# A graph layer with residual norm on one core: product chunks spread over the row schedule, u prepared in pieces, last products in three pieces

## The chip, the core and the metric

The kernel runs on one core of a Trainium2 chip. TensorE does matmuls and transposes into PSUM; VectorE, ScalarE and GpSimd work on data in SBUF and, the first two, in PSUM; SyncE and ScalarE issue DMAs. The metric is the device time of one execution in microseconds (us).

## What is computed

For each of 8 batches, with N = 2048 nodes and C = 64 channels (the adjacency `W` is 2048 x 2048 in float32, 16 MB per batch):

```python
Ws = 0.5 * (W + jnp.swapaxes(W, -1, -2))
A = jax.nn.sigmoid(U @ U.T)              # U: 2048 x 16, one for all batches
K = Ws * A[None, :, :]
deg = jnp.maximum(K.sum(axis=-1), EPS)
d = jax.lax.rsqrt(deg)
K = K * d[:, :, None] * d[:, None, :]
g = w_scale * jnp.einsum('bnm,bmc->bnc', K, x)
out = _layernorm(x + g, axis=-1)
```

## The kernel before

**Tiling.** A batch's adjacency is cut into 16 units of 512 x 512 (1 MB); unit (i, j) lies in SBUF as `K[(i, j)]`, 128 partitions x 4 chunks x 512. K is symmetric, so only ten blocks are worked out (`STEPS`: the diagonal ones and those below), of four rows of 128 each: 40 rows per batch, numbered 0 to 39. Rows of a diagonal block are 128, 256, 384 and 512 columns wide, all others 512.

**A row.** For each pair of rows TensorE transposes the mirrored unit into PSUM `tw` (four banks; 16 instructions for a full pair, 6 or 14 on the diagonal; `transpose_adjacency`, line 349). VectorE adds `tw` to the unit (line 572) and, one row behind, multiplies by the gate A and sums the row for the degree (line 583). Six rows later or so, TensorE transposes the finished rows back for the mirrored half into PSUM `kt` (two banks, line 362, both used by each pair of rows), and ScalarE copies them out with their row sums (line 489: a copy of 0.6 us and a readout of the sum). The next `kt` transposes wait for these copies (`upper_done`); those of a block's first two rows also wait for VectorE to be done with the block (`lower_done`).

**Products.** When the degrees of a group of nodes are known (`DEG_ROWS`, a power on GpSimd) and x is scaled by d (`Z_ROWS`, tile z), TensorE multiplies: eight pairs of units (`PAIRS`), each with four chunks, and a chunk is two matmuls over 512 columns, of 64 x 512 outputs side by side, each of which runs as two instructions. The 32 chunks of a batch accumulate in the two banks of `yp`. The output is copied, transposed, scaled, x is added, and mean, centring, square, variance and division make the norm, in four parts on GpSimd, beside the rows of the following batches.

**What sets the order.** Each engine runs a list written out by row. Tables of clocks say where each piece of side work stands: a clock c of batch b means row c mod 40 of batch b + c // 40. So `PRODUCT_ROWS` = 41 is row 1 of the next batch. On TensorE a row holds, in this order, the `tw` transposes (even rows), the y transposes, the products of that row, and the `kt` transposes (even rows). The first batch has in addition, per two rows, three outer products of u with three sigmoids (lines 416 and 480), which make the gate A that stays in SBUF.

**Loads.** SyncE's queue loads the next batch's units pair by pair; a pair's load waits until the pair's last product is done (`prod_done`, line 215), since the products are the last readers. Rows 4, 12, 16 and 28 are the first to add into (1,0), (2,0), (3,0) and (3,2). `STORE_PAIR` says behind which pair's loads the output store of the batch before the previous one stands.

**Start and end.** Before row 0, u is split into high and low parts in `stack_a` and `stack_b` (lines 698 and 704) and transposed in eight groups through eight PSUM banks (line 452), copied by VectorE and ScalarE (709, 546). After the last batch's row 39 TensorE does what is left of the products (line 469): pairs whose last chunk has a clock of 40 or more. Bank 0 is finished first, and its norm (`finish_last`, lines 662 to 690) runs while bank 1's products are done; bank 1's norm then runs alone.

## Time and profile before

| | us |
|---|---|
| median of three runs | 531.81 (526.47 to 533.03) |
| the profiled execution | 527.15 |
| its span in the profile | 525.3 |
| TensorE busy | 433.0 (82%) |
| VectorE busy | 421.1 (80%) |
| ScalarE busy | 210.2 (40%) |
| GpSimd busy | 118.4 (23%) |
| DMA | 143.08 MB, mean 272 GB/s |

The span leaves out 1.85 us of the execution's time. Busy times are those in which at least one instruction of the engine runs; a matmul's end is modelled, so TensorE's busy share is somewhat too large. A row of the timeline gives start, duration, engine, line, operation, output and input tiles, shapes and count, and in square brackets how long the engine had stood idle before it and what released it.

### The profile page before, as it was taken

Reading aid. Unit: us, or ns where it says so; the run is one execution under the profiler, and the core shown is the slowest. Engines: PE = TensorE matmul, PEld = TensorE weight load, DVE = VectorE, ACT = ScalarE, POOL = GpSimd, SP = SyncE. Lnnn points to the kernel's source line nnn. Section 1 sums busy time; section 2 is a strip of 40 time slices with the busy share of each in tenths; the row PEclk is TensorE's granted clock in tenths of the full one; section 3 lists DMA queues with packets and bytes.
Section 4 is the critical chain, followed back from the end, with each engine's and each line's share of the span. In section 5 each row is a group of like instructions: output and inputs, shape, how many; then the busy total and the mean of one; then the engine's idle time right before and its main releaser. Section 6 shows DMA issues by size and latency. Waiting matters only on the chain.

```text
span 525.3 us, 14322 instructions
## 1 busy us (share of the span) xinstructions
PE 433.0 (82%) x5256; PEld 235.8 (45%) x5256; DVE 421.1 (80%) x1137; ACT 210.2 (40%) x654; POOL 118.4 (23%) x132
## 2 busy tenths in 40 slices
PE   4887789787888789798888789788898889787791
PEld 4555434454445443554345434454354544554230
DVE  5788746999779978999779968899779977999333
ACT  3697421454224531453234531453234541454200
POOL 0000000004410254004410244004410244004611
PEclk9799899999999999999999989999999999999797
DMA  8996569984999689994999669995999679990011
GB/s 281 387 356 240 182 230 365 353 264 168 351 381 285 202 298 357 338 337 167 329 393 307 222 239 353 340 340 190 325 384 309 224 278 371 339 326 0 1 41 40
DMA packets 102857, 143.08 MB, mean 272 GB/s; under 512 B 37296, under 2 KB 37296, under 8 KB 102832
## 3 DMA queue, kind: packets, MB, share of 16 engines
q1 hardware_dynamic: 88240, 139.08, 75.1%
q10 hardware_dynamic: 14592, 3.67, 3.3%
q8 instruction: 16, 0.26, 0.2%
q14 instruction: 9, 0.07, 0.1%
HBM read 138.54 MB, written 4.19 MB: 272 GB/s over the span
## 4 chain that ended last, share of the span: by engine, by line
PE 60%; ACT 11%; issue 10%; DMA 9%; DVE 7%; SPq 1%; POOLq 0%; POOL 0%; DVEq 0%; ACTq 0%
PE yp L387 35%; PE kt L345 13%; ACT k L489 9%; DMA out_dram<-h 7%; PE tw L345 7%; PE yp L469 3%; DVE k L572 2%; DVE k L583 2%; PE yp L416 2%; DMA k<-in_adj_dram 2%; ACT gate L480 1%; SPq L203 1%; DMA h<-in_L_gnn_U_dram 1%; DVE h L619 1%; PE tw L452 1%
## 5 line engine op out<-in xcount | busy, mean ns | idle before, releaser
L489 ACT ACTIVATE k<-kt 128x512 f32<-128x512 f32 (+3 forms) x288 | 149.6, 524 | 266.3 <-PE kt L345 266.2
L572 DVE TENSOR_TENSOR k<-tw,k 128x512 f32<-128x512 f32 (+2 forms) x320 | 193.3, 604 | 66.2 <-PE tw L345 56.2
L387 PE MATMUL yp<-k,z 128*64 128x512 f32 x928 | 219.5, 610 | 0.6 <-issue 0.4
L583 DVE CUSTOM_DVE_ANT_0 k<-k,gate 128x512 f32<-128x512 f32 (+2 forms) x320 | 202.4, 633 | 0.3 <-ACT gate L480 0.3
L345 PE MATMUL kt<-ident,k 64*128 64x64 f32 x1920 | 93.5, 229 | 70.7 <-ACT k L489 61.5
L345 PEld LDWEIGHTS kt<-ident,k 64*128 64x128 f32 x1920 | 76.2, 140 | 99.7 <-issue 99.4
L387 PEld LDWEIGHTS yp<-k,z 128*64 128x64 f32 x928 | 61.3, 139 | 100.3 <-issue 95.8
L345 PEld LDWEIGHTS tw<-ident,k 64*128 64x128 f32 x2176 | 82.7, 140 | 49.9 <-issue 49.8
L345 PE MATMUL tw<-ident,k 64*128 64x64 f32 x2176 | 100.2, 228 | 1.7 <-DMA k<-in_adj_dram 0.9
L277 POOL TENSOR_TENSOR d<-deg,minus_half 128x4 f32<-128x4 f32 x32 | 34.3, 1071 | 254.4 <-DVE deg L593 254.2
L489 ACT ACTIVATION_READ_ACCUMULATOR k<-kt 128x1 f32 x288 | 57.2, 199 | 0.0
L253 POOL TENSOR_TENSOR h<-h,x_keep 128x256 f32<-128x256 f32 x28 | 24.0, 880 | 52.6 <-DVE deg_parts L583 52.6
L265 POOL TENSOR_TENSOR rstd<-var,minus_half 128x16 f32<-128x16 f32 x7 | 20.3, 2899 | 23.2 <-DVE var L633 23.2
L583 DVE DVE_READ_ACCUMULATOR2_ANT deg_parts<- 128x1 f32 x320 | 25.5, 80 | 0.0
L259 POOL TENSOR_TENSOR h<-h,mean 128x256 f32<-128x256 f32 x28 | 19.3, 696 | 26.6 <-DVE deg_parts L583 15.0
L469 PE MATMUL yp<-k,z 128*64 128x512 f32 x96 | 23.5, 650 | 0.0
L270 POOL TENSOR_TENSOR h<-h,rstd 128x256 f32<-128x256 f32 x28 | 17.0, 612 | 26.3 <-DVE deg_parts L583 26.2
L480 ACT ACTIVATE gate<-yp 128x512 f32<-128x512 f32 (+3 forms) x40 | 19.9, 535 | 4.4 <-PE yp L416 4.2
L416 PE MATMUL yp<-ut_b,ut_a 128*128 128x512 f32 (+3 forms) x40 | 16.6, 470 | 2.0 <-ACT gate L480 1.7
L603 DVE TENSOR_TENSOR z<-xt,d 128x256 f32<-128x256 f32 x32 | 15.5, 484 | 2.3 <-POOL d L277 2.2
L469 PEld LDWEIGHTS yp<-k,z 128*64 128x64 f32 x96 | 7.2, 149 | 14.8 <-issue 14.7
L669 DVE TENSOR_TENSOR k<-tw,f 128x512 f32<-128x512 f32 x2 | 1.4, 692 | 14.3 <-PE tw L398 14.3
(60 smaller groups left out, 130.4 us busy)
## 6 DMA issues: line engine op xcount, KB each, us to landing
k<-in_adj_dram SPq DMA_DIRECT2D x128, 1024.0 KB, 7.2
xt<-in_x_dram ACTq DMA_DIRECT2D x7, 512.0 KB, 5.9
out_dram<-h SPq DMA_DIRECT2D x7, 512.0 KB, 8.9
xt<-in_x_dram SPq DMA_DIRECT2D x1, 512.0 KB, 13.9
out_dram<-k SPq DMA_DIRECT2D x2, 256.0 KB, 2.6
h<-in_L_gnn_U_dram SPq DMA_DIRECT2D x1, 128.0 KB, 3.9
ws<-in_L_gnn_w_scale_dram ACTq DMA_DIRECT2D x1, 0.5 KB, 3.3
```

Source lines behind the costliest of these rows:

```text
L253: nc.gpsimd.tensor_tensor(h[:, part(k), :], h[:, part(k), :], x_keep[:, part(k), :], ALU.add).then_inc(h_ready, 1)
L259: nc.gpsimd.tensor_tensor(h[:, part(k), :], h[:, part(k), :], per_row(mean, part(k).start, part(k).stop), ALU.add).then_inc(centered, 1)
L265: nc.gpsimd.tensor_tensor(rstd[:, :], var[:, :], minus_half[:, :], ALU.pow).then_inc(rstd_ready, 1)
L277: nc.gpsimd.tensor_tensor(d[:, s], deg[:, s], minus_half[:, s], ALU.pow).then_inc(d_ready, 1)
L345: t = pe.transpose(dst[h][:, at + k * H:at + (k + 1) * H], block[H * h:H * h + H, :], ident[H * h:H * h + H, H * h:H * h + H])
L387: t = pe.matmul(yp[at:at + C, m // 2, :], z[:, n * G + c, :], K[(n, m)][:, c, :], start=(q == first_unit[m] and c == 0), stop=(q == last_u ...
L416: pe.matmul(yp[:, g % 2, 0:w], ut_a[:, (i * G + r) * P:(i * G + r + 1) * P], ut_b[:, j * UW:j * UW + w], start=True, stop=True).then_inc(u ...
L469: t = pe.matmul(yp[at:at + C, m // 2, :], z[:, n * G + c, :], K[(n, m)][:, c, :], start=False, stop=(q in (LAST_BANK0 - 1, NQ - OWN - 1) a ...
L480: nc.scalar.activation(A[:, A_AT[g]:A_AT[g] + w], yp[:, g % 2, 0:w], ACT.Sigmoid).then_inc(gate_ready, 1)
L489: nc.scalar.activation(K[(j, i)][:, r, c0:UW].rearrange("p (c h e) -> p c h e", h=2, e=H), whole_rows(kt[:, 0:2, :], r % 2, (UW - c0) // P ...
L572: nc.vector.tensor_tensor(row, whole_rows(tw[:, tw_bank[g] // 2 * 2:tw_bank[g] // 2 * 2 + 2, :], g % 2, w // P), row, ALU.add).then_inc(su ...
L583: nc.vector.tensor_tensor_reduce(row, row, A[:, A_AT[g]:A_AT[g] + w], 1.0, 0.0, ALU.mult, ALU.add, deg_parts[:, i * G + r, j:j + 1]).then_ ...
```

## The change

1. `PRODUCT_ROWS`: the 32 chunks stood in ten places (rows 29, 31, 37, 41, 45, 48, 53, 57, 62, 64); now in nineteen: 29, 32, 33, 35, 38, 39, 42, 44, 45, 46, 47, 50, 52, 54, 56, 59, 61, 64 and 65. The last chunk of pairs 0 to 7 moves from 31, 37, 41, 45, 48, 48, 57, 64 to 32, 35, 39, 45, 46, 52, 56, 65. The other tables of clocks move by up to five rows, `KEEP_ROW` (which also issues the next x load) by six, and the store stands behind pair 5's loads.
2. u is loaded with four neighbouring rows in each partition (256 bytes in a piece instead of 64), split quarter by quarter, and only the first quarter is transposed ahead of row 0; the others stand at rows 0, 1 and 2 of the first batch, all through `kt`. Fourteen transposes of the identity stand first on TensorE, one sigmoid of one column first on ScalarE.
3. Three pairs instead of two end before clock 40, so five instead of six are left for the end. They are done in three pieces: bank 0; the first half of bank 1's columns; the second half, which goes to a `kt` bank and is added to the copied earlier sum. Each piece has its own norm and two stores, the last on two queues.

```diff
-PRODUCT_ROWS = [29, 29, 31, 31, 37, 37, 37, 37, 41, 41, 41, 41, 45, 45, 45, 45, 45, 45, 48, 48, 48, 48, 48, 48, 53, 53, 57, 57, 62, 62, 62, 64]
-DEG_ROWS = [25, 34, 40, 43]
-Z_ROWS = [26, 37, 43, 45]
-KEEP_ROW = 61
+PRODUCT_ROWS = [29, 29, 32, 32, 33, 33, 35, 35, 38, 38, 39, 39, 42, 44, 44, 45, 45, 45, 46, 46, 46, 47, 50, 52, 54, 56, 56, 56, 59, 61, 64, 65]
+DEG_ROWS = [25, 32, 40, 43]
+Z_ROWS = [26, 35, 43, 44]
+KEEP_ROW = 55
...
-STORE_PAIR = 6
+STORE_PAIR = 5
...
+UT_ROWS = [0, 0, 1, 2]
+WARM = 14
...
+PIECES = [(0, 0, G), (1, 0, G // 2), (1, G // 2, G)]
+PIECE_Y_AFTER = 5
...
-            sp.dma_start(u_sb, u.rearrange("(n p) r -> p n r", p=P)).then_inc(h_moved, 16)
+            sp.dma_start(u_sb, u.rearrange("(g p n) r -> p g n r", p=P, n=G)).then_inc(h_moved, 16)
...
+            def transpose_u(k):
+
+                pe.wait_ge(stack_ready, 1 if k == 0 else 2)
+                for e, src in ((2 * k, stack_a), (2 * k + 1, stack_b)):
+                    if e - KT_RING >= 0:
+                        before = e - KT_RING
+                        pe.wait_ge((ut_a_copied, ut_b_copied)[before % 2], before // 2 + 1)
+                    for n in range(G):
+                        t = pe.transpose(kt[:, e % KT_RING, n * P:(n + 1) * P], src[:, k, n, :], ident[:, :])
+                    t.then_inc(ut_done, 1)
...
+            for k in range(WARM):
+                pe.transpose(tw[:, k % TW_RING, 0:P], ident[:, :], ident[:, :])
+            transpose_u(0)
             steps(0, 1)
...
+            for piece, (k, c0, c1) in enumerate(PIECES):
+                columns = slice(c0 * P, c1 * P)
+                chunks = [(pair, c) for pair in LAST_PAIRS[k] for c in range(G)]
+                for at, (pair, c) in enumerate(chunks):
+                    if piece and at == PIECE_Y_AFTER:
+                        transpose_last_y(piece - 1)
+                    if piece == 0 and c == 0 and PAIRS.index(pair) in Z_OF_PAIR:
+                        pe.wait_ge(z_ready, NZ * (B - 1) + (Z_OF_PAIR[PAIRS.index(pair)] + 1))
                     for n, m in pair:
...
+                        half = (m % 2) * C
+                        y = last_sums(piece)[half:half + C, :]
+                        t = pe.matmul(y, z[:, n * G + c, :], K[(n, m)][:, c, columns],
+                                      start=(c0 > 0 and at == 0), stop=(at == len(chunks) - 1))
+                t.then_inc(last_done, 1)
+            transpose_last_y(len(PIECES) - 1)
...
+            act.wait_ge(ident_ready, 1)
+            nc.scalar.activation(warm[:, :], ident[:, 0:1], ACT.Sigmoid)
+            copy_u(0)
...
+            def join_last_y(piece):
+
+                dve.wait_ge(last_done, piece + 1)
+                dve.wait_ge(y_copied, 2 * B - 2 + piece)
+                y = piece_of(K[(0, 0)], piece)
+                nc.vector.tensor_tensor(y, last_sums(piece), y, ALU.add).then_inc(y_copied, 1)
```

Two places on TensorE show the move. The first is rows 32 to 38 of a steady batch: `tw` and `kt` are the two kinds of transposes, `yp<-k,z` are products, four instructions in this list being two chunks of two matmuls. Before:

```order
L345 MATMUL tw<-ident,k 128x64 x6
L345 MATMUL kt<-ident,k 128x64 x16
L345 MATMUL tw<-ident,k 128x64 x14
L345 MATMUL kt<-ident,k 128x64 x16
L345 MATMUL tw<-ident,k 128x64 x6
L345 MATMUL kt<-ident,k 128x64 x16
L387 MATMUL yp<-k,z 64x512 x8
```

and of the change:

```order
L395 MATMUL tw<-ident,k 128x64 x6
L437 MATMUL yp<-k,z 64x512 x4
L395 MATMUL kt<-ident,k 128x64 x16
L437 MATMUL yp<-k,z 64x512 x4
L395 MATMUL tw<-ident,k 128x64 x14
L395 MATMUL kt<-ident,k 128x64 x16
L437 MATMUL yp<-k,z 64x512 x4
L395 MATMUL tw<-ident,k 128x64 x6
L395 MATMUL kt<-ident,k 128x64 x16
```

Three groups of two chunks now stand between and beside the `kt` transposes that followed each other before, and the group of four chunks of row 37 is gone (it has become those of rows 33 and 35).

The second is the end, after the loop: the last `kt` transposes, the products (with `64x256` half as wide) and the y transposes (`tw<-ident,k 128x128`). Before:

```order
L345 MATMUL kt<-ident,k 128x64 x14
L469 MATMUL yp<-k,z 64x512 x28
L398 MATMUL tw<-ident,k 128x128 x4
L469 MATMUL yp<-k,z 64x512 x20
L398 MATMUL tw<-ident,k 128x128 x4
```

and of the change:

```order
L395 MATMUL kt<-ident,k 128x64 x14
L535 MATMUL yp<-k,z 64x512 x16
L535 MATMUL yp<-k,z 64x256 x10
L449 MATMUL tw<-ident,k 128x128 x4
L535 MATMUL yp<-k,z 64x256 x14
L535 MATMUL kt<-k,z 64x256 x10
L449 MATMUL tw<-ident,k 128x128 x2
L535 MATMUL kt<-k,z 64x256 x14
L449 MATMUL tw<-ident,k 128x128 x2
```

The 48 matmuls over 512 columns have become 16 over 512 and 48 over 256, and what follows the last of them has half the columns.

## Rows read from the trace of the kernel before

**Rows 1.** The page, part 1: busy us (share of the span) xinstructions.
```profile
PE 433.0 (82%) x5256; PEld 235.8 (45%) x5256; DVE 421.1 (80%) x1137; ACT 210.2 (40%) x654; POOL 118.4 (23%) x132
```

**Rows 2.** Waits over the span: us in total, times, longest.
```profile
PE kt L345 <- ACT k L489: 61.5, 71, 1.4
DVE k L572 <- PE tw L345: 56.2, 42, 5.2
...
DVE k L572 <- DMA k<-in_adj_dram: 9.5, 13, 1.9
```

**Rows 3.** Busy time by stretch of one steady batch, rows 32 to 15, then 16 to 31.
```profile
core 0: us, PE busy (x) PEld busy (x) DVE busy (x) ACT busy (x) POOL busy (x), PEclk, DMA share, GB/s
359.16:395.87 36.71, 31.23 (x364) 15.74 (x362) 30.04 (x89) 12.65 (x45) 14.88 (x16) 1.00 0.91 330
395.87:417.59 21.72, 19.09 (x295) 11.64 (x292) 21.34 (x54) 10.79 (x31) 1.01 (x1) 1.00 0.82 263
```

**Rows 4.** Timeline, VectorE's adds of rows 10, 12, 29 and 30.
```profile
387.80 0.56 DVE L572 TENSOR_TENSOR k<-tw,k 128x384 f32<-128x384 f32 x1 [1.81 <-PE tw L345]
...
390.45 0.69 DVE L572 TENSOR_TENSOR k<-tw,k 128x512 f32<-128x512 f32 x1 [0.53 <-DMA k<-in_adj_dram]
...
413.95 0.68 DVE L572 TENSOR_TENSOR k<-tw,k 128x512 f32<-128x512 f32 x1
...
415.17 0.68 DVE L572 TENSOR_TENSOR k<-tw,k 128x512 f32<-128x512 f32 x1
```

**Rows 5.** Timeline, TensorE and its weight loads (PEld) at six places.
```profile
381.75 5.37 PE L387 MATMUL yp<-k,z 128*64 128x512 f32 x24
...
387.05 0.14 PEld L345 LDWEIGHTS kt<-ident,k 64*128 64x128 f32 x2 [0.81 <-issue]
...
396.79 0.58 PEld L345 LDWEIGHTS tw<-ident,k 64*128 64x128 f32 x16 [0.81 <-issue]
...
397.37 0.61 PEld L345 LDWEIGHTS kt<-ident,k 64*128 64x128 f32 x16
...
419.14 0.71 PE L345 MATMUL kt<-ident,k 64*128 64x64 f32 x16 [1.01 <-ACT k L489]
...
421.31 0.72 PE L345 MATMUL kt<-ident,k 64*128 64x64 f32 x16 [1.26 <-ACT k L489]
...
421.95 3.65 PE L387 MATMUL yp<-k,z 128*64 128x512 f32 x16
```

**Rows 6.** A 2 us stretch of full loading (columns as rows 3).
```profile
376.00:378.00 2.00, 2.00 (x12) 0.65 (x10) 1.58 (x6) 0.00 (x0) 2.00 (x1) 1.00 1.05 409
```

**Rows 7.** Line 203, the adjacency loads, from issue to landing.
```profile
DMA to landing us min/median/max: 5.0/7.2/16.3
```

**Rows 8.** The page, part 6: the load of u, KB, median us to landing.
```profile
h<-in_L_gnn_U_dram SPq DMA_DIRECT2D x1, 128.0 KB, 3.9
```

**Rows 9.** Timeline of the start, ScalarE.
```profile
12.62 1.28 ACT L480 ACT_TABLE_LOAD   x1
...
13.92 0.55 ACT L480 ACTIVATE gate<-yp 128x128 f32<-128x128 f32 x2
```

**Rows 10.** The stretch from 490 to 500 us (columns as rows 3).
```profile
490.00:500.00 10.00, 10.00 (x36) 2.98 (x37) 2.21 (x6) 1.24 (x3) 6.23 (x6) 0.76 0.01 2
```

**Rows 11.** Timeline of the end.
```profile
489.82 14.71 PE L469 MATMUL yp<-k,z 128*64 128x512 f32 x56
...
491.58 0.24 PEld L469 LDWEIGHTS yp<-k,z 128*64 128x64 f32 x2 [0.62 <-issue]
...
494.93 0.14 PEld L469 LDWEIGHTS yp<-k,z 128*64 128x64 f32 x2 [0.55 <-issue]
...
509.82 4.03 PE L469 MATMUL yp<-k,z 128*64 128x512 f32 x18
...
515.25 0.69 DVE L669 TENSOR_TENSOR k<-tw,f 128x512 f32<-128x512 f32 x1 [2.86 <-PE tw L398]
...
519.99 1.64 POOL L327 TENSOR_TENSOR rstd<-var,minus_half 128x8 f32<-128x8 f32 x1 [8.32 <-DVE var L687]
```

More of the change, by code:

```diff
@@ L88, in upper_row_of @@
     return (s + 1) * G + r + UPPER_LAG
+FIRST_STEP_OF_ROWS = [min(s for s in range(len(STEPS)) if STEPS[s][0] == i) for i in range(G)]
 def gates_before(row):
@@ L98, in due @@
     return clock == NL * lag + row
-LAST_PAIRS = [n for n in PAIRS[OWN:] if n[0][1] == 0] + [n for n in PAIRS[OWN:] if n[0][1] != 0]
-LAST_BANK0 = sum(n[0][1] == 0 for n in PAIRS[OWN:])
-LAST_Y_CHUNK = 2
+LAST_PAIRS = [[n for n in PAIRS[OWN:] if n[0][1] // 2 == k] for k in range(2)]
+PIECES = [(0, 0, G), (1, 0, G // 2), (1, G // 2, G)]
+PIECE_Y_AFTER = 5
 def bass_graph_resnorm_kernel(nc, x, adj, u, w_scale, out):
@@ L382, in product @@
                         pe.wait_ge(gate_ready, NL)
-                    elif q < 2 and not first:
-                        pe.wait_ge(y_scaled, 2 * b + (q - 1))
+                    elif q in FIRST_PAIR_OF_BANK and not first:
+                        pe.wait_ge(y_scaled, 2 * b + (FIRST_PAIR_OF_BANK.index(q) - 1))
                 for n, m in PAIRS[q]:
@@ L437, in steps @@
                     if lags == 1:
+                        for k in range(1, G):
+                            if UT_ROWS[k] == row:
+                                transpose_u(k)
                         for g in range(gates_before(row), gates_before(row + 1)):
@@ L534, in steps @@
                     if lags == 1:
+                        for k in range(1, G):
+                            if UT_ROWS[k] == row:
+                                copy_u(k)
                         for g in range(gates_before(row), gates_before(row + 1)):
@@ L654, in steps @@
                     add_row(b, g)
+                    if lags == 1:
+                        for k in range(1, G):
+                            if UT_ROWS[k] == g:
+                                copy_u(k)
                     if g:
@@ L693, in _ @@
             nc.vector.memset(deg_parts[:, :, :], 0.0)
[L694 to L695 removed]
+            nc.vector.memset(stack_a[:, :, :, 4 * R:P], 0.0)
+            nc.vector.memset(stack_b[:, :, :, 4 * R:P], 0.0)
             dve.wait_ge(h_moved, 16)
[L697 to L698 removed]
@@ L711, in _ @@
+            copy_u(0)
             steps(0, 1)
@@ L729, in _ @@
             dve.wait_ge(f_ready, B)
-            for k in range(2):
-                finish_last(k)
+            for piece in range(len(PIECES)):
+                if PIECES[piece][1] > 0:
+                    join_last_y(piece)
+                last_center(piece)
+                if piece:
+                    last_divide(piece - 1)
+                last_var(piece)
+            last_divide(len(PIECES) - 1)
 _INS = ["x", "adj", "L0_gnn_U", "L0_gnn_w_scale"]
```

212 lines of the change are left out of this document (122 added, 90 removed).

## The prediction

> **What bounds the kernel now.** The page first: TensorE is busy for 82% of the 525.3 us span and VectorE for 80% [rows 1]; neither is a plain bound, so the waits come next. Over the span TensorE waits 61.5 us for ScalarE's copies out of kt, VectorE 56.2 us for TensorE's tw and 9.5 us for adjacency loads [rows 2]. The two engines wait for each other, at different places. I then cut one steady batch out by VectorE's rows, from its first add of row 32 to the same add a batch later: 58.43 us, VectorE busy 51.38, TensorE 50.32 (the sums of the two stretches in [rows 3]). In rows 16 to 31 (21.72 us) VectorE is busy 21.34: that stretch is VectorE's own work. In row 32 to row 15 of the next batch (36.71 us) VectorE is busy 30.04 and idles 6.67. So any gain in steady state must come out of these 6.67 us; below 51.4 us a batch VectorE is the bound.
>
> The timeline says who takes them [rows 4]: 1.81 us at row 10, behind the 24 product matmuls of row 8, and 0.53 us at row 12 for a load; four such waits for TensorE and two for loads make up the stretch. On TensorE the same stretch has three kt transposes in a row at rows 32, 34 and 36 with nothing but 14 or 6 short transposes between them; each stands about 1.0 to 1.3 us until ScalarE has emptied kt [rows 5]. So TensorE idles first and is overloaded directly after: the products stand in few, large groups at the wrong places.
>
> **What the change does, part by part.**
>
> *Products.* A chunk (four matmul instructions) is worth 0.86 us: the group of 24 starts at 381.75 and the next kt weight load at 387.05, 5.30 us for six [rows 5]; so a group costs 0.86 per chunk and about 0.14 once for leaving it. Entering costs about 0.1: from a kt group to its product group 0.64 us pass (421.31 to 421.95), from one transpose group of 16 to the next 0.58 or less (396.79 to 397.37). The change makes 19 groups out of 10, so TensorE gets 9 x 0.25 = 2.2 us more to do per batch, 50.3 -> 52.5.
>
> Against that stand the waits for ScalarE, 8 us in this batch (the two in [rows 5] are of nine). In the new order two chunks stand between the kt groups of rows 30, 32, 34 and 36, and one chunk or more ahead of those of rows 2, 6, 10 and 14. ScalarE needs about 1.4 us for two rows of kt (419.14 + 0.71 to 421.31); two chunks and a tw group take more, so these waits go, all but a few tenths at row 8.
>
> I walk stretch 32 to 16 with these prices: 0.55 per 16 transposes (0.22 and 0.48 for 6 and 14), 0.86 per chunk, the 0.25 per group, 1.21 us of VectorE per full row (413.95 to 415.17, [rows 4]), VectorE's small operations at their new rows, and TensorE ahead by some 3 us at row 32 (it has 1.1 us of work in rows 30 and 31, against 3.0 before). TensorE then reaches the tw of row 34 at 2.0 us (VectorE stands 0.2), of row 36 at 4.7 (0.5), of row 0 at 10.3 (1.0), of row 6 at 18.5 (none), of row 8 at 23.0 (1.3). VectorE begins row 12 at 26.4 and, unhindered, row 16 at 31.2.
>
> *Loads.* A unit of 1 MB takes 2.6 us at the 409 GB/s of a full stretch [rows 6]; from the data's start to the first unit's landing it is 3.6 us, and from issue about 1.5 us more (the shortest landing is 5.0, [rows 7]). The new places free pair 0 a row later, pairs 1, 2 and 4 two rows sooner, pair 5 four rows later. By the walk (1,0) lands at 15.1 us, when row 4 wants it at 14.8 (stall 0.35); (2,0) lands at 26.4, just when row 12 starts. But (3,0) is freed by the chunk at row 12, at 27.2; it lands at 32.3, and row 16 wants it at 31.2: a new stall of 1.1 us. These stalls add up to 4.4 us. VectorE's work in the stretch is 27.9 us by unit prices (eight full rows 9.7, four diagonal blocks of 3.2, small operations 5.4), 30.0 by the trace [rows 3]; the difference is time in which GpSimd works beside it, and part of that will fall into the stalls. So row 16 comes between 32.3 us (all of it absorbed) and 34.4 (none); I take 33.6, nearer the second, since the measured stretch is the sum of both (30.0 + 6.7). Gain 36.7 - 33.6 = **3.1 us per batch, 21.7 for seven**.
>
> Rows 16 to 31 stay at 21.7: VectorE has the same work there. (3,2) is freed at row 25 instead of 24 and needed at row 28, 6.3 us of VectorE's work later against 5 to 5.5 to landing: no cost, without much left. The output store moves ahead of the loads of pair 6: SP waits there for the divide of row 14, two rows ahead of pair 6's last product, so nothing behind it on SP is late. The x load, now issued at row 15 from ScalarE's queue, comes after (3,0) has its data.
>
> *The start.* Before, all eight groups of u transposes and their copies stand ahead of row 0, and ScalarE loads its sigmoid table only then, at 12.62, for 1.28 us, with the first gate behind it at 13.92 [rows 9]. Now only the first quarter of u is split and transposed ahead of row 0, and the table is loaded while u is on its way. VectorE still splits all four quarters before the first copy: 4 + 12 operations of half the old size, 3.3 us (0.2 each, a quarter of the 0.69 for 512 columns in [rows 11] and a little) after u has landed, 3.9 us from its issue at the start [rows 8], then the copy; the first gate comes at about 10.5 instead of 13.9 us, but three more pairs of u copies now stand among the first gates. I take **2.7 us**, with 1 and 4 as bounds (only the table; the whole shift of the gate).
>
> *The end.* The third pair is now done at row 39: four chunks leave the last product run and go where VectorE is still busy with rows 38 and 39: 4 x 0.86 = 3.4 us. The last run now begins with a pair that needs the third z, which was done just as TensorE began that run before (489.82, [rows 11]), so that costs nothing. Before, the run's first passes follow each other in 0.86 us (0.24 and 0.62 idle, [rows 11]), against 0.43 at full clock (5.16 us for twelve in [rows 5]); the granted clock is 0.76 over 490 to 500 [rows 10], after a stretch in which TensorE did little but short transposes and waits. Until 494.93 that costs 5.1 - 2.5 = 2.6 us. Now TensorE has product work until about 2.5 us before that run, so I expect most of it saved, 2.4. From the last product to the end of the span 11.45 us pass (513.85 to 525.3: copy, transposes, VectorE operations of 0.69, square, a pow of 1.64, store [rows 11]). With half the columns the VectorE operations and the square halve (7 x 0.35 = 2.4), the pow falls (bounds 0.8 and 1.64; I take 1.1, 0.5 less), and the joining add replaces the longer copy (0.2): 3.1 us. Half-width passes cost half each: the same 12 chunks twice at 0.43. Sum of the end: 3.4 + 2.4 + 3.1 = 8.9 us, with 0.2 back for two more interruptions of the run and 0.5 gained since row 38, and so z, comes earlier: **9.2 us**.
>
> **The rule that speaks against it.** The trace shows 0.25 us per change between transposes and products, as above [rows 5]. 
>
> **Sum.** 2.7 + 21.7 + 9.2 = 33.6 us off the profiled execution: 527.15 - 33.6 = 493.6. The three runs' median, 531.81, lies 4.7 above that execution and the lowest 0.7 below it; I forecast 494, near the undisturbed executions.
>
> **The rivals.**
> - *Dear changes.* If each change costs what stands idle on the weight load after a product group, 0.81 us [rows 5], nine more cost 7.3 us per batch: TensorE 50.3 + 7.3 = 57.6, a gain of 0.8 a batch, 5.6 in all: 527.15 - 5.6 - 11.9 = 510. Against it: the group of 24 leaves only 0.14 unexplained. This is where the tiling rule would end. Chance 0.12.
> - *Late pair 5: slower.* (3,0) and (3,1) are freed at row 12 and wanted at rows 16 and 24. A batch is 27.2 + landing + 21.7. At the forecast's 5.1 us that is within the sum; at the longest landing of the trace, 16.3 us [rows 7], it is 65.2: seven times 6.8 slower, less 11.9, so 563. It is not faster by 2% from a landing of about 10 us on, and slower by 2% from about 13. Against it: the median landing is 7.2 [rows 7] with two units queued, and by row 12 the queue is nearly empty. Chance 0.04.
> - *All waits go.* Leads absorb the small stalls and a batch falls to VectorE's 51.4: 7 x 7.0 + 11.9 = 61 us, 466. Against it the load of (3,0) and 52.5 us of TensorE work. Chance 0.06.
> - *The end does not shrink.* If half-width passes took as long as whole ones, twelve chunks more at 0.86 = 10.3: 504. No product before has 256 columns. Chance 0.05.
> - *Small steady gain.* The order moves waits rather than removing them, 1 us a batch: 508. For it: VectorE idles 6.67 now and still 4.4 in my walk, and a few tenths wrong per row pair eat the rest. Chance 0.10.
>
> **How the numbers follow.** Forecast 0.63, own range 484 to 503. The range 480 to 512 takes in dear changes, the small gain and the long end, and leaves out the slow case, the full cover and accidents. The cases below about 521 hold 0.96; 0.05 of it I give to accidents within 2%. Faster by over 2% 0.91, within 2% 0.05, slower 0.04; 2% is about what a measurement of this kernel can tell from no change.
>
> **What would show it.** TensorE's waits for ScalarE at kt falling from 61.5 us to below 25; VectorE's waits for tw from 56.2 to about 30; its waits for adjacency loads rising from 9.5 to some 15, at row 16; a batch of 55 to 56 us; the first gate before 11.5 us; about 8.2 us from last product to end; the last run at full clock. If the batch stays above 57.5, or TensorE's busy time per batch rises by more than 4 us, the price per group was wrong.

## The result

The changed kernel takes 489.77 us (median of 4 runs, 487.63 to 492.27) against 531.58 us for the kernel before beside it (526.47 to 533.03): a ratio of 0.9231, with a 95% interval of 0.9156 to 0.9307. The profiled execution took 489.78 us, with a span of 487.9. Forecast were 494 us. Some executions, of either kernel, come out longer at a lower granted clock (up to 501 us at 0.95 below); they stand in the ranges, and the ratios leave them out. Two more sessions with the unaltered changed kernel gave ratios of 0.9200 (0.9106 to 0.9294) and 0.9206 (0.9151 to 0.9261).

The page of the changed kernel, part 1, answers to [rows 1]:

```profile
PE 447.6 (92%) x5318; PEld 236.5 (48%) x5318; DVE 417.0 (85%) x1154; ACT 209.9 (43%) x655; POOL 113.4 (23%) x133
```

TensorE's share has gone from 82% to 92%: it does 14.6 us more and has 37.4 us less span to do it in. Its waits and VectorE's (us in total, times, longest), for [rows 2]:

```profile
DVE k L666 <- PE tw L395: 28.5, 35, 6.2
PE kt L395 <- DVE deg_parts L677: 13.5, 20, 2.4
DVE k L666 <- DMA k<-in_adj_dram: 13.4, 17, 2.1
DVE deg L685 <- ACT k L559: 10.3, 12, 1.3
PE kt L395 <- ACT k L559: 5.3, 10, 1.1
```

TensorE's wait for ScalarE, 61.5 us before, is 5.3; VectorE's wait for tw has halved; its wait for loads has grown. New are VectorE's waits for a copy of ScalarE ahead of a batch's degrees (`deg`, 2.1 before), and grown are TensorE's at `kt` for VectorE's product with the gate (13.5, 3.8 before).

To see where the 37.4 us are, I cut both executions in three: at VectorE's first add of row 32 of the first batch and of the last. These adds stand in the kernel before here:

```profile
60.52 0.29 DVE L572 TENSOR_TENSOR k<-tw,k 128x128 f32<-128x128 f32 x1 [1.90 <-PE tw L345]
...
476.34 0.28 DVE L572 TENSOR_TENSOR k<-tw,k 128x128 f32<-128x128 f32 x1
```

and in the changed kernel at 59.70 and 449.14. Busy time in the three stretches (columns as in [rows 3]), before:

```profile
0.00:60.52 60.52, 44.49 (x504) 30.54 (x506) 43.85 (x113) 37.27 (x94) 1.78 (x8) 0.92 0.83 289
60.52:476.34 415.82, 356.00 (x4552) 192.62 (x4548) 355.00 (x968) 163.06 (x531) 98.18 (x106) 0.99 0.86 299
476.34:525.30 48.96, 32.56 (x214) 12.60 (x210) 22.21 (x58) 9.83 (x29) 18.45 (x18) 0.86 0.10 22
```

and after:

```profile
0.00:59.70 59.70, 48.84 (x508) 32.36 (x508) 43.98 (x121) 36.07 (x94) 1.79 (x8) 0.86 0.84 293
59.70:449.14 389.44, 369.31 (x4560) 189.57 (x4560) 349.45 (x970) 164.78 (x534) 95.95 (x109) 0.99 0.92 320
449.14:487.90 38.76, 29.47 (x256) 14.57 (x252) 23.55 (x67) 9.10 (x28) 15.69 (x16) 0.94 0.12 28
```

So the start gives 0.8 us, the seven steady batches 26.4, the end 10.2. In the steady stretch TensorE is busy 13.3 us longer, which is 95% of it. The two control traces put the steady gain at 32.5 and 22.8 us (383.3 and 393.1 instead of 415.8) and the end's at 8.5 each, so a single trace fixes neither term better than that.

The starts of VectorE's adds cut a steady batch further. Mean us of a stretch over the seven steady batches, for the kernel before and for three traces of the changed one (the first, and those of the two control runs below):

```
rows            32 to 0   0 to 8   8 to 12   12 to 16   16 to 32   sum
before           11.08    14.09     6.53       5.68      22.03    59.41
changed, 1st     10.08    13.02     4.66       5.86      22.02    55.64
changed, 2nd     10.04    12.94     4.48       5.57      21.73    54.76
changed, 3rd     10.09    13.05     5.01       6.18      21.82    56.15
```

In the first trace one us is gained ahead of row 0, 1.1 in rows 0 to 7 and 1.9 in rows 8 to 11, and rows 12 to 15 lose 0.2. In the other two rows 8 to 11 gain 2.0 and 1.5, and rows 12 to 15 gain 0.1 and lose 0.5. The changed kernel has short and long batches. A short one (from 226.50) and a long one (from 280.05), each cut at row 16:

```profile
226.50:258.35 31.85, 31.68 (x358) 14.69 (x353) 28.54 (x89) 12.44 (x43) 11.82 (x13) 1.00 1.01 372
258.35:280.05 21.70, 20.25 (x296) 12.03 (x296) 21.67 (x52) 11.13 (x35) 3.16 (x4) 1.00 0.86 277
280.05:314.52 34.47, 32.97 (x376) 15.45 (x371) 28.53 (x88) 13.26 (x45) 11.82 (x13) 1.00 1.02 368
314.52:337.22 22.70, 20.34 (x276) 11.80 (x278) 21.84 (x52) 10.29 (x32) 3.16 (x4) 0.92 0.72 226
```

In the short batch TensorE is busy for 31.68 of the 31.85 us from row 32 to row 15, then VectorE for 21.67 of 21.70. One engine or the other is busy nearly throughout, and none of the 21 batches of the three traces takes less than 53.46 us. The long batch takes 57.17, 3.62 more, mostly by three loads: VectorE waits 1.25 us instead of 0.31 at row 12, 2.12 instead of 0.44 at row 16 and 0.35 at row 28 (and 0.48 for tw at row 20). The largest is that of row 16:

```profile
258.35 0.69 DVE L666 TENSOR_TENSOR k<-tw,k 128x512 f32<-128x512 f32 x1 [0.44 <-DMA k<-in_adj_dram]
...
314.52 0.69 DVE L666 TENSOR_TENSOR k<-tw,k 128x512 f32<-128x512 f32 x1 [2.12 <-DMA k<-in_adj_dram]
```

and, from the chain of work that ended last (start, us, what), the load of (3,0) that each waits for:

```profile
253.09 5.14 DMA k<-in_adj_dram
...
306.65 7.76 DMA k<-in_adj_dram
```

Both were issued 26.6 us after row 32; one landed in about the shortest time known (5.0 in [rows 7]), the other took 2.6 us longer.

### The profile page after: what moved, and what is told of

It is laid out like the page before. It is cut to its first block, busy times and chain, and to the rows that moved or that the text cites. A ratio compares the mean times of both kernels' runs of the same rounds, so it can differ in the third digit from the quotient of the medians.

```text
span 487.9 us, 14490 instructions
## 1 busy us (share of the span) xinstructions
PE 447.6 (92%) x5318; PEld 236.5 (48%) x5318; DVE 417.0 (85%) x1154; ACT 209.9 (43%) x655; POOL 113.4 (23%) x133
## 4 chain that ended last, share of the span: by engine, by line
PE 61%; DMA 14%; DVE 12%; issue 8%; ACT 2%; SPq 1%; POOL 0%; DVEq 0%; POOLq 0%
PE yp L437 35%; DMA k<-in_adj_dram 14%; PE tw L395 10%; PE kt L395 9%; DVE k L666 6%; DVE k L677 3%; PE yp L535 3%; PE yp L470 2%; ACT k L559 1%; ACT gate L546 1%; SPq L251 1%; DVE deg_parts L677 1%; DMA h<-in_L_gnn_U_dram 1%; PE kt L481 1%; PE kt L535 0%
## 5 line engine op out<-in xcount | busy, mean ns | idle before, releaser
L437 PE MATMUL yp<-k,z 128*64 128x512 f32 x944 | 239.6, 615 | 4.9 <-DVE z L697 2.6
L677 DVE CUSTOM_DVE_ANT_0 k<-k,gate 128x512 f32<-128x512 f32 (+2 forms) x320 | 198.5, 620 | 0.0
L395 PE MATMUL kt<-ident,k 64*128 64x64 f32 x1920 | 94.2, 232 | 19.5 <-DVE deg_parts L677 13.5
L437 PEld LDWEIGHTS yp<-k,z 128*64 128x64 f32 x944 | 56.4, 137 | 73.1 <-issue 60.0
L327 POOL TENSOR_TENSOR d<-deg,minus_half 128x4 f32<-128x4 f32 x32 | 32.5, 1015 | 222.1 <-DVE deg L687 221.4
L559 ACT ACTIVATION_READ_ACCUMULATOR k<-kt 128x1 f32 x288 | 57.2, 198 | 0.0
L309 POOL TENSOR_TENSOR h<-h,mean 128x256 f32<-128x256 f32 x28 | 17.7, 633 | 46.0 <-DVE deg_parts L677 46.0
L303 POOL TENSOR_TENSOR h<-h,x_keep 128x256 f32<-128x256 f32 x28 | 20.9, 757 | 31.3 <-DVE deg_parts L677 31.3
L697 DVE TENSOR_TENSOR z<-xt,d 128x256 f32<-128x256 f32 x32 | 13.8, 430 | 2.3 <-POOL d L327 2.2
L685 DVE TENSOR_REDUCE deg<-deg_parts 128x4 f32<-128x20 f32 x32 | 5.4, 169 | 10.3 <-ACT k L559 10.3
L535 PE MATMUL yp<-k,z 128*64 128x256 f32 (+1 forms) x80 | 12.5, 467 | 0.1
L567 ACT ACTIVATE y_sb<-yp 128x512 f32<-128x512 f32 x14 | 8.4, 599 | 5.3 <-ACT x_keep L579 5.3
```

Source lines behind the costliest of these rows:

```text
L303: nc.gpsimd.tensor_tensor(h[:, part(k), :], h[:, part(k), :], x_keep[:, part(k), :], ALU.add).then_inc(h_ready, 1)
L309: nc.gpsimd.tensor_tensor(h[:, part(k), :], h[:, part(k), :], per_row(mean, part(k).start, part(k).stop), ALU.add).then_inc(centered, 1)
L327: nc.gpsimd.tensor_tensor(d[:, s], deg[:, s], minus_half[:, s], ALU.pow).then_inc(d_ready, 1)
L395: t = pe.transpose(dst[h][:, at + k * H:at + (k + 1) * H], block[H * h:H * h + H, :], ident[H * h:H * h + H, H * h:H * h + H])
L437: t = pe.matmul(yp[at:at + C, m // 2, :], z[:, n * G + c, :], K[(n, m)][:, c, :], start=(q == first_unit[m] and c == 0), stop=(q == last_u ...
L535: t = pe.matmul(y, z[:, n * G + c, :], K[(n, m)][:, c, columns], start=(c0 > 0 and at == 0), stop=(at == len(chunks) - 1))
```

## The experiments

### The tables alone

The kernel before, with the changed tables of clocks, `KEEP_ROW` and `STORE_PAIR`; its own start and its own two last pieces.

```diff
-PRODUCT_ROWS = [29, 29, 31, 31, 37, 37, 37, 37, 41, 41, 41, 41, 45, 45, 45, 45, 45, 45, 48, 48, 48, 48, 48, 48, 53, 53, 57, 57, 62, 62, 62, 64]
-DEG_ROWS = [25, 34, 40, 43]
+PRODUCT_ROWS = [29, 29, 32, 32, 33, 33, 35, 35, 38, 38, 39, 39, 42, 44, 44, 45, 45, 45, 46, 46, 46, 47, 50, 52, 54, 56, 56, 56, 59, 61, 64, 65]
+DEG_ROWS = [25, 32, 40, 43]
...
-STORE_PAIR = 6
+STORE_PAIR = 5
```

> The kernel before with only the tables of clocks of the change (products, degrees, z, copies, the norm's steps, the store behind pair 5). The start and the two last pieces over 512 columns stay as before; since three pairs now end before clock 40, the last run has five pairs. By the terms of the prediction: 21.7 us for seven batches, 3.4 for the four chunks moved, 2.4 for the full clock and 0.5 for the earlier z, so 527.15 - 28.0 = 499 us. By the trace of the changed kernel (55.63 us between two rows 32 instead of 59.40): 26.4 instead of 21.7, so 494. Rival (the steady gain needs the new start, because the loads of the first batches set its phase): 505 or more.

Measured: 496.99 us (495.41 to 500.78), ratio 0.9432 (0.9325 to 0.9540) to the kernel before beside it. In its trace row 32 of the first batch comes at 60.75, the seven batches take 391.2 us and the end 41.6. So the steady gain (24.6 us) needs neither the new start nor the pieces, and the rival falls. The moved third pair, the clock and the earlier z bring 7.3 us at the end (48.96 to 41.6), where I had 6.3. The time, 497, lies between the two that were expected, 499 and 494.

### The new start alone

The kernel before, with the u load, split, transposes and copies of the changed kernel.

```diff
+UT_ROWS = [0, 0, 1, 2]
+WARM = 14
...
-            for k, (dst, bank) in enumerate(UT_BANKS):
...
+            for k in range(WARM):
+                pe.transpose(tw[:, k % TW_RING, 0:P], ident[:, :], ident[:, :])
+            transpose_u(0)
```

> The kernel before with only the new start (u in quarters, first quarter ahead of row 0, identity transposes, sigmoid table first). Theory A, the prediction's term: 2.7 us less, 524.5. Theory B, from the trace of the changed kernel: VectorE's first add comes 5.7 us sooner (7.56 instead of 13.30), but row 32 of the first batch only 0.8 sooner (59.70 instead of 60.52), so 0.8 less, 526, and the lead is lost between rows 16 and 32. Rival C: nothing absorbs the lead in this kernel, whose batches are longer anyway, and 5.7 us come through: 521.5.

Measured: 527.94 us (521.89 to 534.27, 10 runs), ratio 0.9885 (0.982 to 0.995), which is 2.7 to 9.6 us. The trace says otherwise: first add at 7.75, row 32 of the first batch at 60.97, the batches 417.4 and the end 49.2 us, a span of 527.6 against 525.3. That trace is of an execution of 529.45 us, one of the longer ones of this run; the kernel before spreads over 527.5 to 538.5 us in that session, so one trace against one trace cannot decide it. By the times the start is worth something in this kernel (6 us in the middle of the interval, with the 2.7 of theory A at its edge, the 5.7 of C inside it and the 0.8 of B outside); the trace does not show where.

### Two pieces instead of three

```diff
-PIECES = [(0, 0, G), (1, 0, G // 2), (1, G // 2, G)]
+PIECES = [(0, 0, G), (1, 0, G)]
```

> The changed kernel with the last products in two pieces, bank 0 and bank 1, both over 512 columns, instead of three. The prediction's term for the half-width last piece is 3.1 us, less 0.2 for interruptions: so 2.9 slower than the changed kernel, 492.7. Rival: the pieces are worth nothing because the extra weight loads and the joining add eat it: 490. Rival: half-width passes run slower than half (then two pieces would be faster than the changed kernel, below 489).

Measured: 494.24 us (491.46 to 494.75), ratio 0.9361 (0.9330 to 0.9393); end of its trace 41.66 us against 38.76 with three pieces, 2.9 longer. On TensorE and GpSimd the last bank reads

```profile
471.85 6.23 PE L535 MATMUL yp<-k,z 128*64 128x512 f32 x28
...
484.21 1.64 POOL L377 TENSOR_TENSOR rstd<-var,minus_half 128x8 f32<-128x8 f32 x1 [5.74 <-DVE var L799]
```

and with three pieces, in the changed kernel,

```profile
461.16 9.25 PE L535 MATMUL yp<-k,z 128*64 128x512 f32 x52
470.34 0.66 PE L449 MATMUL tw<-ident,k 128*128 128x128 f32 x4
470.93 3.24 PE L535 MATMUL yp<-k,z 128*64 128x256 f32 x28
...
476.63 3.24 PE L535 MATMUL kt<-k,z 128*64 128x256 f32 x28
...
484.06 1.01 POOL L377 TENSOR_TENSOR rstd<-var,minus_half 128x4 f32<-128x4 f32 x1 [3.11 <-DVE var L799]
```

28 matmuls over 512 columns take 6.23 us, 28 over 256 take 3.24: half, and 0.12 more for all 28. From the last product's end to the end of the span 11.5 us pass with two pieces (489.6 - 478.1) and 8.0 with three (487.9 - 479.9). The run of products and y transposes itself is 18.1 us with two and 18.7 with three. 3.5 gained and 0.6 given back make the 2.9 of the forecast, whose parts were 3.1 and 0.2. The times say more: 494.24 is 4.5 us above the 489.77 of the changed kernel, which was not run beside it, and the ratios (0.9361 and 0.9231) differ by 7 us. What lies beyond 2.9 is not in this trace, whose batches (389.3) and first batch are like the changed kernel's.

All but the start is alike in this kernel and in that of the tables alone: the same tables, two last pieces, ends of 41.66 and 41.64 us. So 494.24 beside 496.99, measured together, is one more measure of the new start: 2.7 us, with overlapping intervals (0.9330 to 0.9393, and 0.9325 to 0.9540); in the traces row 32 of the first batch comes at 58.61 and 60.75.

### Pair 5 free sooner

```diff
-PRODUCT_ROWS = [... 46, 46, 46, 47, 50, 52, 54, ...]
+PRODUCT_ROWS = [... 46, 46, 46, 47, 48, 50, 54, ...]
```

> The changed kernel with the last two chunks of pair 5 at clocks 48 and 50 instead of 50 and 52, so that units (3,0) and (3,1) are free one chunk group earlier. In the trace of the changed kernel their load is issued 26.6 us after row 32 in every batch, lands 5.1 to 7.8 us later, and VectorE waits for it at row 16: 0.44 us in four batches, 2.1 and 1.9 in two. Theory (this load ends last in each batch): each batch gains the 1 us by which the load is issued sooner as far as row 16 stalls, between 0.44 and 1.1, so 484 to 487. Rival (TensorE is the bound in rows 32 to 15, busy 31.7 of 31.9 us in the batch from 226.50, and the chunk ahead of the tw transposes of row 10 delays them by 0.86): 490 or slower.

Measured: 487.86 us (485.47 to 490.31), ratio 0.9239 (0.9126 to 0.9352); the seven batches took 386.2 us. The three traces of the changed kernel have 389.4, 383.3 and 393.1, so no gain can be told. The waits at row 16 are 0.37 to 1.27 us instead of 0.34 to 2.12. Neither theory is shown: 487.86 lies between the 487 of one and the 490 of the other.

### The changed kernel again

> The changed kernel once more, unaltered, as the measure for the three beside it and as a second trace. Expected as before: 488 to 492 us; from row 32 of the first batch to row 32 of the last 389.4 us, row 32 of the first batch at 58.6 to 61 us. If VectorE's waits for the load of (3,0) at row 16 fall on other batches than in the first trace (2.1 and 1.9 us in the sixth and the eighth), they come from the loads' own spread and not from the place in the program.

Measured: 488.75 us (483.73 to 492.57, 6 runs). The batches took 383.3 us, and the waits at row 16 were 0.43 to 1.13: the sixth and the eighth batch are short here. So the long batches come from the loads' spread, not from a fixed place in the program; what makes a load land late is open.

### Products back to row 37

```diff
-PRODUCT_ROWS = [29, 29, 32, 32, 33, 33, 35, 35, 38, 38, 39, 39, ...]
+PRODUCT_ROWS = [29, 29, 31, 31, 37, 37, 37, 37, 38, 38, 39, 39, ...]
```

> The changed kernel with the six chunks of rows 32, 33 and 35 back at 31 and 37 (two and four), so that three kt groups stand at rows 32 to 36 with no product between them. Theory A (the gain comes from products that cover ScalarE's copies): TensorE waits there again, 1.01 + 1.26 us as before the change and somewhat more, and since TensorE is the bound from row 32 to row 15 (31.7 us busy of 31.9) this comes through: 2 to 3 us a batch, 504 to 511 us, TensorE's waits for ScalarE at kt above 20 us. Rival B (only the spread of rows 2 to 12 matters, TensorE catches up in the rest): within 3 us of the changed kernel.

Measured: 523.61 us (522.95 to 526.31), ratio 0.9884: 34.9 us slower than the changed kernel beside it. Its seven batches take 420.4 us, 37.1 more, and rows 32 to 0 take 14.9 instead of 10.0 each; all other stretches are within 0.2 us of the changed kernel's. Theory A has the direction, but half the price or less (504 to 511 us). TensorE's waits for ScalarE rose by 10.5 us only, against the 5.9 of the control beside it, and stay below the 20 of theory A; VectorE's for tw rose from 21.6:

```profile
DVE k L666 <- PE tw L395: 64.8, 33, 5.6
...
PE kt L395 <- ACT k L559: 16.4, 20, 1.2
```

What costs is the group of four chunks at row 37, with those of rows 38 and 39 behind it, where VectorE's rows are short (128 to 384 columns):

```profile
302.56 1.12 PE L395 MATMUL kt<-ident,k 64*128 64x64 f32 x16 [1.24 <-ACT k L559]
303.61 6.03 PE L437 MATMUL yp<-k,z 128*64 128x512 f32 x16
309.57 0.66 PE L395 MATMUL tw<-ident,k 64*128 64x64 f32 x14
...
310.26 0.56 DVE L666 TENSOR_TENSOR k<-tw,k 128x384 f32<-128x384 f32 x1 [4.36 <-PE tw L395]
```

The same group of 16 matmuls takes 3.65 us at full clock [rows 5]. Here it takes 6.03, 4.6 to 6.2 in all eight batches: TensorE stood idle behind ScalarE just before, and the granted clock around it is

```profile
300.00:310.00 10.00, 8.36 (x67) 3.83 (x68) 5.83 (x22) 2.53 (x8) 2.45 (x3) 0.66 0.49 188
```

The clock can be priced: over the seven batches TensorE is busy for 383.2 us here and for 366.7 in the control, with the same matmuls, so 16.6 of the 37.1 us are work that ran slower. The rest is idle time, TensorE's at kt and behind VectorE. That the waits at kt bring the clock down is not shown: the kernel before has such waits ahead of this group too (1.01 and 1.26 us in [rows 5], the 1.26 in every batch), and there six of the eight groups take 3.65 us, the others 5.04 and 5.35.

Nor does the whole gain hang on these six chunks. The kernel before has them in the same places and needs 11.08 us for rows 32 to 0, not 14.9; there the next four chunks stand at row 41 and not at 38 and 39. So this run shows that chunks at rows 38 and 39 need the others at rows 32 to 35: with eight chunks in rows 37 to 39 that stretch is slower than in either kernel.

### Products of the rows 42 to 52 back to 45 and 48

```diff
-PRODUCT_ROWS = [..., 42, 44, 44, 45, 45, 45, 46, 46, 46, 47, 50, 52, ...]
+PRODUCT_ROWS = [..., 45, 45, 45, 45, 45, 45, 48, 48, 48, 48, 48, 48, ...]
```

> The changed kernel with the twelve chunks of pairs 3, 4 and 5 back at clocks 45 and 48, six each, instead of in seven places from 42 to 52. Theory A: at row 10 VectorE waits for tw behind the group of 24 matmuls as before the change (1.81 us instead of 0), and kt waits for ScalarE return at rows 2 and 6; against it five groups fewer (0.18 us each, by TensorE's busy time of 51.9 instead of 50.3 us for nine groups more) and pair 5 freed at row 8, so no wait at row 16 (0.4 to 2.1 us). Sum +0.5 to +2 a batch: 493 to 504 us. Rival B (dear changes of mode: fewer groups are better): below 488. Rival C (the load of pair 5 is what limits): 480 to 487.

Measured: 494.36 us (489.57 to 497.20), 5.6 slower than the changed kernel beside it, though the intervals of the ratios, 0.9176 to 0.9391 and 0.9106 to 0.9294, overlap. Stretch by stretch theory A is right in both directions: rows 8 to 12 take 6.4 us instead of 4.5, with the wait behind the group of 24 back,

```profile
314.49 0.56 DVE L666 TENSOR_TENSOR k<-tw,k 128x384 f32<-128x384 f32 x1 [1.75 <-PE tw L395]
```

and rows 0 to 8 take 11.9 in most batches instead of 12.8; TensorE waits 13.6 us for ScalarE at kt instead of 5.9. Fewer changes between transposes and products do not pay (B had the kernel below 488): rival B falls. So does C, with its 480 to 487, although the wait it would remove is gone: rows 12 to 16 take 4.9 to 5.4, as in a short batch.

### The old start in the changed kernel

```diff
-UT_ROWS = [0, 0, 1, 2]
-WARM = 14
...
-            for k in range(WARM):
-                pe.transpose(tw[:, k % TW_RING, 0:P], ident[:, :], ident[:, :])
-            transpose_u(0)
+            for k, (dst, bank) in enumerate(UT_BANKS):
...
-            nc.scalar.activation(warm[:, :], ident[:, 0:1], ACT.Sigmoid)
```

> The changed kernel with the start of the kernel before (all u transposes ahead of row 0, sigmoid table at 12.6 us); everything else as changed. Theory A (the early gates are eaten up before row 32 of the first batch, which every trace so far has at 58.6 to 61 us, whatever the start): 0 to 1 us slower than the changed kernel, about 490. Theory B, the prediction's term: 2.7 slower, 492.5. Theory C: the whole shift of the first add comes through, 5.7 slower, 495.5.

Measured: 488.01 us (485.10 to 501.18), ratio 0.9202 (0.9092 to 0.9313), where the changed kernel beside it has 488.75 and 0.9200. The first add comes 5.4 us later, but row 32 of the first batch comes a little sooner. Here, and below it in the second trace of the changed kernel:

```profile
13.13 0.62 DVE L625 TENSOR_TENSOR k<-tw,k 128x128 f32<-128x128 f32 x2 [1.03 <-PE tw L382]
...
57.22 0.29 DVE L625 TENSOR_TENSOR k<-tw,k 128x128 f32<-128x128 f32 x1
```

```profile
58.17 0.28 DVE L666 TENSOR_TENSOR k<-tw,k 128x128 f32<-128x128 f32 x1
```

With the old start rows 0 to 8 of the first batch take 9.5 us, with the new one 12.1: the u pieces now lie among the first gates, and 2.6 us of the lead go there. The rest goes in rows 16 to 32, 24.4 us against 28.2: VectorE waits there at row 30 for tw, 2.20 us with the old start and 5.48 with the new one, behind the break of TensorE that the next section is about. Over all traces, row 32 of the first batch comes at 57.2, 60.5 and 60.8 with the old start and between 56.8 and 61.0 in eleven with the new one (mean 59.0, against 59.5). So theory C falls, in this kernel, and most of the lead is lost within the first batch, as A says. Between A's 0 to 1 us and B's 2.7 the times do not decide: each of the two ratios has an interval of 10 us or more.

### No identity transposes

```diff
-WARM = 14
+WARM = 0
```

> The changed kernel without the fourteen transposes of the identity at TensorE's start (their results are read by nobody). Theory A (the hole in the first product group of the first batch is TensorE waiting for its next 16 KB of instructions): everything behind it stands 28 instructions nearer to the start of the stream, so the end of that 16 KB piece falls 14 matmuls later, behind the product group and among the tw transposes of row 30; the products cover most of the fetch, VectorE's wait at row 30 (6.2 us in the first trace, 5.5 in the second) falls by 2 to 3 us, row 32 of the first batch comes at 56 us or sooner, and the kernel takes 485 to 487. Rival B (the hole is a wait for data or for the gates): it stays in its place, and the kernel takes as long as the changed one. Rival C (the transposes keep the clock up): without them the first u transposes run at half clock, the first gate comes 0.5 us or more later and the time is 1 us longer.

Measured: 488.10 us (486.62 to 491.44), ratio 0.9198 (0.9149 to 0.9248), against 490.84 and 0.9206 for the changed kernel beside it: the same. But the hole moved. In the second trace of the changed kernel TensorE stands still at two places of the first batch, and goes on each time about 2 to 3 us behind a 16 KB packet on the instruction queue (the packets fall between 35 and 36 and between 49 and 50 us):

```profile
36.82 0.59 PE L395 MATMUL tw<-ident,k 64*128 64x64 f32 x12
38.18 0.34 PE L395 MATMUL tw<-ident,k 64*128 64x64 f32 x4 [0.77 <-issue]
...
47.43 1.07 PE L437 MATMUL yp<-k,z 128*64 128x512 f32 x2
51.67 3.40 PE L437 MATMUL yp<-k,z 128*64 128x512 f32 x6 [3.17 <-issue]
```

Without the fourteen transposes:

```profile
39.48 0.46 PE L395 MATMUL kt<-ident,k 64*128 64x64 f32 x8 [0.40 <-issue]
43.10 0.69 PE L395 MATMUL kt<-ident,k 64*128 64x64 f32 x8 [3.17 <-issue]
...
56.10 0.46 PE L395 MATMUL tw<-ident,k 64*128 64x64 f32 x7
56.88 0.52 PE L395 MATMUL tw<-ident,k 64*128 64x64 f32 x9 [0.32 <-issue]
```

The second break stood after two of eight matmuls; now it stands after seven of the sixteen tw transposes that follow the group: 6 + 7 = 13 matmuls later. The first stood after 12 of 16 and now stands after the other 4, one outer product and 8 of the next kt: 13 again. The packets fall between 40 and 41 and between 54 and 55 us now. Theory A said 14, so one matmul is unaccounted for in both. In all ten traces that have the new start with its fourteen transposes the two breaks stand in the same places, whatever else was changed. Rival B, a wait for data or gates, would have left them there in this run too; the stream of instructions moves like this. That is theory A, and its price was wrong: the second hole shrank to 0.32, as expected, but the first grew from 0.77 to 3.17, and row 32 came at 59.86. Rival C's part is seen too. The first two groups of four u transposes take 0.86 and 0.60 us in the first trace, 1.12 and 1.02 in the second, and all later ones 0.60 to 0.66; here five groups take 1.05 to 1.09 each, and the first gate comes at 10.26 us instead of 9.37 to 9.62. The time does not show it.

### Clock 42 emptied

```diff
-PRODUCT_ROWS = [..., 39, 39, 42, 44, 44, 45, ...]
+PRODUCT_ROWS = [..., 39, 39, 44, 44, 44, 45, ...]
```

> The changed kernel with the one chunk of clock 42 moved to clock 44. At clock 42 it stands ahead of the kt transposes of that row, ScalarE's copy comes later by its 0.86 us, and VectorE waits 0.91 us for it in every batch before the degrees of row 3 (rows 0 to 7 take 12.81 us; in the run with the products of rows 42 to 52 in their old places they took 11.88). Theory A (VectorE's waits add up): this wait goes, 0.9 us a batch, 6 us in all: 483. Rival B (the stream of adjacency loads sets the pace of rows 8 to 16: from row 12 to row 16 5.40 us pass in nearly every batch, which is two units of 1 MB at 390 GB/s, and the loads are freed by TensorE's products, which do not come sooner): VectorE only waits longer at row 12, and the time stays within 2 us of the changed kernel.

Measured: 492.95 us (488.57 to 496.38), ratio 0.9248 (0.9188 to 0.9309), beside 490.84: no gain, and rows 0 to 8 take 13.7 us in most batches instead of 12.8. The time is B's, the mechanism neither's. I had taken the wrong copy: VectorE's wait at `deg` is for the kt rows behind the group of clock 44, not for those of clock 42. With a third chunk in that group it got longer (15.3 us in total, 9.7 in the trace of the changed kernel beside it), and TensorE now waits where the chunk stood:

```profile
293.50 0.53 PE L395 MATMUL kt<-ident,k 64*128 64x64 f32 x10 [0.68 <-DVE deg_parts L677]
...
298.53 0.17 DVE L685 TENSOR_REDUCE deg<-deg_parts 128x4 f32<-128x20 f32 x1 [1.76 <-ACT k L559]
```

The one chunk of clock 42 filled a gap of TensorE. A chunk taken out of a gap cost its whole 0.86 us here (13.67 us for rows 0 to 8 instead of 12.81).

### Four chunks at 44, pair 5 sooner

```diff
-PRODUCT_ROWS = [..., 42, 44, 44, 45, 45, 45, 46, 46, 46, 47, 50, 52, ...]
+PRODUCT_ROWS = [..., 44, 44, 44, 44, 45, 45, 46, 46, 46, 47, 48, 50, ...]
```

> The changed kernel with the chunks of clocks 42, 44, 44, 45 all at 44 and the last two of pair 5 at 48 and 50: pair 3's units and pair 5's units are free sooner, by the tw group and the small kt group between (about 0.8 us) and by 1 us. Theory B of the run beside it (the loads set the pace): rows 8 to 16 shorten by 0.5 to 1 us a batch, beside the 0.9 of clock 42, so 3 to 9 us: 480 to 486. Rival (tw of rows 6 and 10 comes too late now): no gain, 488 or more.

Measured: 491.47 us (487.21 to 495.72), ratio 0.9211 (0.9151 to 0.9270), beside 490.84. The rival holds. By its trace, of an execution of 495.04 us and so one of the longer ones, VectorE waits 8.3 us in all for loads instead of 20.2 in the control beside it, but 23.0 for the copies ahead of the degrees instead of 9.7, and the batches take 394.5 us. No version here beats the changed kernel.

### The third control

> The changed kernel unaltered, as the measure for the three beside it and as a third trace. 484 to 492 us; in rows 16 to 31 of the first batch TensorE again stands about 3 us within the first product group (51.00 to 52.86 in the first trace, 3.17 us before 51.67 in the second), just after a packet of the instruction queue (at 50 and 49 us).

Measured: 490.84 us (486.91 to 498.76), batches 393.1 us, row 32 of the first batch at 56.78.

## Why the prediction was right, and where it was not

**What bounds it.** Right: the two engines wait for each other, VectorE's rows 16 to 31 stayed at 21.7 us in a short batch, and the gain lies in rows 32 to 15.

**Products, the price of a group.** The forecast gave TensorE 2.2 us more per batch (0.25 for each of nine groups). Measured: 369.31 - 356.00 = 13.3 us in seven batches, 1.9 each, 0.21 a group (0.17 and 0.19 in the control traces). With larger groups at rows 45 and 48 the time did not fall. "Dear changes" (0.81 each) is refuted; of the drain that the Trainium skill names (TensorEngine Tiling (Array Packing), Key Properties) no more than these 0.17 to 0.21 us is to be seen here.

**Waits for ScalarE.** 61.5 us to "below 25"; it is 5.3. The waits went as forecast. The forecast priced only the waits: in the run with row 37 the batches take 37 us more, of which 10.5 are waits for ScalarE and 16.6 are TensorE's work at a lower clock.

**The walk.** Stretch 32 to 15 was forecast at 33.6 us. Measured: 31.85 in a short batch, 34.47 in a long one, 33.6, 33.0 and 34.3 as means of the three traces. Stall by stretch it was mixed: row 34 had 0.28 for 0.2, row 0 0.64 for 1.0, row 8 0.56 for 1.3, row 16 0.44 to 2.12 for 1.1; not foreseen were 0.91 us at the degrees of row 3 and the load at row 12 (0.3 to 1.6). The sum, 4.4, lies between VectorE's idle time in the short batch, 3.3 (31.85 - 28.54), and in the long one, 5.9.

**The steady term, 21.7, was mis-sized: 26.4 measured.** The forecast for the changed batch was right (55.3 by its own sum, 33.6 + 21.7; measured 55.63), the batch that it was taken from was not typical. I cut out one batch of 58.43 us [rows 3]; the seven take 415.82, 59.40 each. 0.97 a batch was thus there to be lost, and 0.67 of it in rows 32 to 15, where the mean is 37.38 and not 36.71. 7 x 0.67 = 4.7, which is the miss against this trace. Against the control traces the miss would be 10.8 and 1.1, so this account, too, fits only as well as one trace of either kernel can carry.

**Loads.** The stall at row 16 came where it was forecast, at the least landing in the short batches. VectorE's wait for loads is 13.4 us for "some 15" (12.9 and 20.2 in the control traces). The late-pair rival is the long batch in small: landings of 6.4 to 8.6 us cost up to 2.6. None of the loads of (3,0) that the chains of the three traces show took 10 us or more, where it would have decided.

**The start, 2.7: the step behind it failed, its size is open.** The first gate came at 9.37 instead of "about 10.5", and VectorE's first add 5.7 us sooner than before. The step that failed is that a lead at row 0 is a lead at the end: of these 5.7 us 0.8 are left at row 32 of the first batch in this trace. The forecast named the u copies among the first gates and gave them no price; they take 2.6 us back by row 8, and the break of TensorE in rows 16 to 31, which the forecast did not know, takes most of the rest. What the start is worth in time came out as about nothing (old start in the changed kernel), 2.7 us (two pieces beside the tables alone) and 2.7 to 9.6 us (new start in the kernel before). So 2.7 is not refuted as a size; if it is right, it is so by luck.

**The end, 9.2: 10.2 in the first trace, 8.5 in both control traces.** Pieces: 2.9 forecast, 2.9 measured; passes over half the columns cost half, so the rival "the end does not shrink" falls. From last product to end: 8.2 forecast, 8.0 measured. The third pair, clock and z: 6.3 forecast, 7.3 measured. The VectorE operations over half the columns took 0.42 us, not 0.35, and the pow 1.01, not 1.1. The clock was the loose part: the last run's first 52 matmuls take 9.25 us in the first trace, at a granted clock of 1.00, and 10.94 in the second, where it is 0.61 up to 456 us:

```profile
453.47 10.94 PE L535 MATMUL yp<-k,z 128*64 128x512 f32 x52
```

So the product work ahead of that run does not always save the clock: TensorE was busy for 10.3 of the 12 us before it in both. The 1.7 us of difference are the spread of the end, 38.8 or 40.4.

**The sum.** 2.7 + 21.7 + 9.2 = 33.6 was forecast, 0.8 + 26.4 + 10.2 = 37.4 measured. A start too dear by 1.9 and a batch and an end too cheap by 4.7 and 1.0 leave 3.8. All this is measured from the profiled execution of the kernel before, 527.15 us, which is 4.4 below its median; from median to median the gain is 41.8 us. That 494 came within 1% of 489.77 is thus better than the terms are.

## What to carry to other kernels

Small pieces of filler work belong where a busy engine would otherwise wait, here for a copy of its own output; a large group behind short rows of the other engine is paid there in full, and here it ran at a lowered clock as well in every batch. Take a steady period from first to last repetition, not from one that looks clean, and from more than one trace. A lead won at the start is worth only what is left of it after the first repetition, so follow it to there before it is put in a sum.

## What was unexpected

- TensorE stands up to 3.2 us in the first batch for what must be its own instructions, at a fixed distance in the instruction stream (13 matmuls later with 14 transposes fewer in front), 2 to 3 us behind a 16 KB packet on the instruction queue. What it costs depends on the work ahead of that point: 0.32 us behind a product group of eight matmuls, 3.17 inside the row's transposes.
- Behind two waits of about 1.0 and 1.2 us with only short transposes between them, a product group of 16 matmuls runs partly at half clock: 4.6 to 6.2 us instead of 3.65 in all eight batches of the run with row 37, and in two of eight in the kernel before. What decides it is open. The granted clock of the seven steady batches is 0.96 in that run and 0.99 to 1.00 in the kernel before and in the changed one.
- The load of (3,0) is issued 26.6 us after row 32, to within 0.02 us, in batches four to seven of the first trace, and lands 5.1 to 7.8 us later. With the load of row 12, which varies too, this makes most of the difference between a batch of 53.6 and one of 57.2 us.
